# Graph network on Trainium2: picking groups of 13, 12, 12 and 12 nodes, and a third buffer for gathered rows

## The chip, the core and the metric

The kernel runs on one NeuronCore of a Trainium2 chip. The metric is the device time of one execution in microseconds; of several runs the median is taken. The engines are PE (matrix multiplication), DVE (vector), ACT (scalar), POOL (here it issues indirect DMAs, that is gathers and scatters by row) and SP (it issues plain DMAs).

## The reference, cut to what matters

Four graph layers work on 6250 nodes with 32 features and 200000 edges sorted by destination, with a residual and a layer norm after each:

```python
x = layernorm(x + L0(x, edge_attr_32))   # relu(x[src] + e), summed by dst
x = layernorm(x + L1(x))                 # softmax attention by cosine, over edges of a dst
x = layernorm(x + L2(x, edge_attr_2))    # spline convolution, 4 corners an edge
x = layernorm(x + L3(x, edge_attr_16))   # five PNA layers: sum, mean and max by dst
```

For this change only one step of L1 and L3 counts: for each edge, fetch a row of a node table, `table[src[e]]`. In L3 one layer of five is

```python
h   = x[dst] @ P + x[src] @ Q + (edge_attr @ eW + eb) @ C + pb   # 32 values an edge
out = [x, mean_dst(h), sum_dst(h), max_dst(h)] @ poW + pob
x   = relu(out @ lW + lb)
```

so the table is `x @ Q` (TQ), 32 wide, new in every layer. In L1 it is x and one over its norm, 33 wide, fetched once.

## The kernel before, in words

Edges lie as 128 partitions by J = 1568 slots. They are worked in NCH = 28 chunks of C = 56 slots, and one slot is 128 edges. Node n has the high digit n // 49 (0 to 127, its partition in tables held on chip) and the low digit n % 49.

**Two ways to fetch.** Of the 56 slots of a chunk POOL fetches the first 36 in the last layer (20 in L1), each with one indirect DMA of 128 rows from HBM (L1775, L1095). The other KP = 20 (KP1 = 36 in L1) are "picked" by PE and DVE from a table on chip:

- The table is split into three bf16 parts that add up to the f32 value (QS, L2003 to L2013; QS1, L1385 to L1394), and its 49 low digits into PG = 4 groups of PH = 13; 4 x 13 = 52, and the three digits too many are zeros. A part of a group is 32 features by 13 digits, 416 columns (33 by 13, 429, in L1).
- DVE makes one-hots (L2023, L1272): for each group a 128x128 matrix for a slot, a one where the edge's key, group x 128 + high digit, is the row's. Keys come by DMA from a table KG, broadcast to all partitions.
- PE multiplies the one-hot of each group with the three parts of the group, 12 matmuls into one PSUM bank (L1862, L1173). An edge has a one in one group only, so the bank then holds, for each edge, 32 features by 13 low digits of its group.
- DVE multiplies by a mask of the low digit within the group (`by_h`, L2032, L1285; the mask is made by `which`, L2076, from hpb) and reduces over the 13 (`together`, L2037, L1291) into the same buffer where the gathered rows land (G3, G1).

Three PSUM banks turn: pick k starts once the reduction of pick k - 3 is done (of pick k - 2 for the first two picks of a chunk).

**Order on each engine in the last layer.** All of it is written out by hand. PE: 20 picks, after picks 13, 15, 17 and 19 two matmuls each for the edge attributes (`mix`, L1872). DVE: for each pick k by_h(k), together(k-1), one-hots for the next ten picks at k = 0, 2, 4, 6 of ten; between them the work on the chunk before: two adds of gathered and picked rows onto the edge sums in PSUM (`add`, L2046) after picks 2 and 4, four half scans for sum and maximum (L2068) after picks 6, 8, 10 and 12, the next mask after pick 16. ACT copies scans out and lays the edge terms. POOL: the gathers of a chunk, before them a wait until the adds of two chunks before are done, since G3 has two buffers. At the end of each of the five layers the rows are stored, gathered by node, and go through small matmuls to the next table; then DVE's `parts` splits it and PE waits for that.

**L1** is the same with 36 picks; DVE puts the steps of `chunk` between picks 1 and 20, `fill` (a 3.96 us scan, L1307) after pick 23 and cell numbers (`cells_v`) after 26 to 33. POOL also scatters 39 rows of another table in each chunk (L1077).

**Keys.** `pick_keys_v` (L1549) runs once, at the end of L0: q_g is the group number of each edge, q_kf = 128 q_g + high digit goes through PE transposes (L509) to KG, hpb = low digit - 13 q_g is the digit within the group.

Of the kernel before, what the change touches and what calls it, by code (L numbers as in the profile page):

```python
# [19 lines left out]
C = 56  # L20
# [5 lines left out]
PG = 4  # L26
PH = 13
KP = 20
# [47 lines left out]
def program(nc, x, src, dst, ea16, ea2, ea32, eps, beta, w2, root2, bias2,  # L76
            eW, eb, pW, pb, poW, pob, lW, lb, out):
    ctx = ExitStack()
    with ctx:
# [172 lines left out]
        with ExitStack() as ph:  # L252
            NB = sb(ph, "l1n", [128, PG * PH, 34])
# [10 lines left out]
            QS1 = sb(ph, "qs1", [128, PG, 3, 33, PH], BF16)  # L264
            QR1 = [O1[i][:, :, :].rearrange("p a b -> p (a b)")[:, 0:PG * PH * 33].rearrange("p (a b) -> p a b", b=33)
# [53 lines left out]
        with ExitStack() as ph:  # L319
            XC = sb(ph, "xc", [128, NC, 32])  # L320
            PN = RX
            G3 = [sb(ph, f"l3g{i}", [128, C, 32]) for i in range(2)]
# [6 lines left out]
                "p (a b) -> p a b", b=128) for i in range(2)] for t_ in G3)  # L329
            XT = [OF[0][0:32, :, :].rearrange("p a b -> p (a b)")[:, 896 * i:896 * i + 896].rearrange(  # L330
                "p (a b) -> p a b", b=128) for i in range(2)]
            QN = OF[1][:, :, :].rearrange("p a b -> p (a b)")[:, 0:PG * PH * 32].rearrange("p (a b) -> p a b", b=32)
            QR = [O3[1][:, 0:52, :].rearrange("p a b -> p (a b)")[:, 1664 * i:1664 * i + 1664].rearrange(
                "p (a b) -> p a b", b=32) for i in range(2)]
            QS = sb(ph, "qs", [128, PG, 3, 32, PH], BF16)
# [16 lines left out]
        def ranked(r):  # L352
# [27 lines left out]
                   + z1.over(root=2, tab=3, hat=1, tabd=16, hatd=16, sl=16 * NCH, lays=NCH, fm=NCH, filled=NCH,  # L380
                             score=2 * NCH, ev=NCH, em=NCH, av=NCH, spread=NCH, prod=NCH, scan=2 * NCH, lay=3 * NCH,
                             o0=16 * 14, o1=16 * 14, cells=NCH, celld=32 * NCH, lastT=2, fa=1, fea=1, fb=1, feb=1,
                             carry=2, carryT=2, oh=NB1 * NCH, pk=KP1 * NCH, pev=KP1 * NCH, red=RED0 + KP1 * NCH, m5=NCH))

# [689 lines left out]

        def send(e, a, b):
# [39 lines left out]
        def layer1_sp(e):  # L1115
# [24 lines left out]
            e.wait_ge(z1["tab"], 3)  # L1140
# [23 lines left out]
        def layer1_t(e):  # L1164
            e.wait_ge(z1["parts"], 1)
            with nc.Fori(0, 2 * NCH, engines=[e.engine], hint_back_edge=True, head_slot={e.engine: 0}) as i:
                for k in range(KH1):
# [3 lines left out]
                    for g in range(PG):  # L1171
                        for p in range(3):
                            x_ = e.matmul(ps[k % 3][:, 0:33 * PH],  # L1173
                                          OH1[k // SB1][:, g, 128 * (k % SB1):128 * (k % SB1) + 128],
                                          QS1[:, g, p, :, :].rearrange("p f h -> p (f h)"),
# [84 lines left out]
        def layer1_v(e, vc):  # L1260
# [107 lines left out]
            e.memset(NB[:, NC:PG * PH, :], 0.0).then_inc(z1["tab"], 1)  # L1368
# [11 lines left out]
            def by_group(t_):  # L1380
                return t_.rearrange("p (g h) f -> p g f h", g=PG)

            NBt = NB[:, :, 0:33]
            e.wait_ge(z1["tab"], 3)
            a = vc.up(e.tensor_copy(QS1[:, :, 0, :, :], by_group(NBt)).then_inc(vec, 1))  # L1385
            e.wait_ge(vec, a)
            a = vc.up(e.tensor_tensor(by_group(QR1[0]), by_group(NBt), QS1[:, :, 0, :, :], ALU.subtract).then_inc(vec, 1))
# [928 lines left out]
```

## Time and profile before

| what | value |
|---|---|
| median of 3 runs | 15540.85 us (15536.74 to 15546.09) |
| the profiled execution: its time, its span | 15539.17 us, 15537.4 us |
| PE matmul busy | 10581.2 us, 68% |
| DVE busy | 10047.1 us, 65% |
| POOL busy | 10665.1 us, 69% |
| ACT busy | 2687.8 us, 17% |
| mean granted TensorE clock | 0.875 of full |

How to read it: the kernel goes through stages with different limits. L1's picking loop is at 2630 to 5068 us of the span, L2 without picks at 5220 to 8100, and the five last layers from 8116 to 15415. Busy shares of the whole span mix them. A busy PE is modelled: each matmul's duration holds its latency, so the step from one start to the next tells the rate.

### The profile page before, as it was taken

Reading aid. Unit: us, or ns where it says so; the run is one execution under the profiler, and the core shown is the slowest. Engines: PE = TensorE matmul, PEld = TensorE weight load, DVE = VectorE, ACT = ScalarE, POOL = GpSimd, SP = SyncE. Lnnn points to the kernel's source line nnn. Section 1 sums busy time; section 2 is a strip of 40 time slices with the busy share of each in tenths; the row PEclk is TensorE's granted clock in tenths of the full one; section 3 lists DMA queues with packets and bytes.
Section 4 is the critical chain, followed back from the end, with each engine's and each line's share of the span. In section 5 each row is a group of like instructions: output and inputs, shape, how many; then the busy total and the mean of one; then the engine's idle time right before and its main releaser. Section 6 shows DMA issues by size and latency. Waiting matters only on the chain. (4 is left out here: it accounts for less than half of the span.)

```text
span 15537.4 us, 159495 instructions
## 1 busy us (share of the span) xinstructions
PE 10581.2 (68%) x59370; PEld 6309.5 (41%) x59370; DVE 10047.1 (65%) x16354; ACT 2687.8 (17%) x3352; POOL 10665.1 (69%) x10775
## 2 busy tenths in 40 slices
PE   0166562999999540000029997999799979988997
PEld 0155551444444220000015554555455545545554
DVE  2799993777777213333337775777577757776776
ACT  0122221010101100000002221222222212221222
POOL 3777666666666777777767775777577667766775
PEclk9999999999999555555559998999899989998998
DMA  5122222111111222222212221222122212221221
GB/s 195 43 63 63 67 60 48 40 44 40 44 40 40 72 82 69 72 73 71 71 46 74 74 75 52 74 74 74 52 74 73 76 54 74 75 68 57 74 74 60
DMA packets 677474, 1029.59 MB, mean 66 GB/s; under 512 B 252382, under 2 KB 526347, under 8 KB 652027
## 3 DMA queue, kind: packets, MB, share of 16 engines
q1 hardware_dynamic: 311483, 763.42, 13.9%
q0 software_dynamic: 344384, 236.12, 7.5%
q10 hardware_dynamic: 21216, 25.94, 0.5%
q14 instruction: 281, 2.30, 0.0%
q8 instruction: 110, 1.80, 0.0%
HBM read 587.57 MB, written 479.53 MB: 69 GB/s over the span
## 5 line engine op out<-in xcount | busy, mean ns | idle before, releaser
L1862 PE MATMUL ps<-qs,oh 128*128 128x416 bf16 x33600 | 6083.2, 340 | 342.0 <-DVE l3g L2037 269.0
L1775 POOL DMA_INDIRECT l3g<-TQ,srcs x5040 | 4835.2, 959 | 1984.4 <-issue 1510.0
L1862 PEld LDWEIGHTS ps<-qs,oh 128*128 128x128 bf16 x33600 | 3242.8, 98 | 3105.9 <-DVE l3g L2037 518.2
L2032 DVE TENSOR_TENSOR pt<-ps,l3m 128x416 f32<-128x416 f32 x2800 | 1635.3, 584 | 1668.4 <-PE ps L1862 1663.6
L1173 PE MATMUL ps<-qs,l1oh 128*128 128x429 bf16 x12096 | 2282.0, 350 | 261.7 <-DVE l1g L1291 156.5
L967 POOL DMA_INDIRECT l0g<-T,srcs x1568 | 1640.5, 1046 | 847.8 <-issue 487.5
L1077 POOL DMA_INDIRECT T<-p,poss x1568 | 1529.6, 976 | 807.8 <-issue 478.7
L1685 POOL DMA_INDIRECT l2g<-Y,t x1568 | 1680.5, 1072 | 489.6 <-issue 489.6
L1173 PEld LDWEIGHTS ps<-qs,l1oh 128*128 128x128 bf16 x12096 | 1183.8, 99 | 1359.6 <-DVE l1g L1291 211.1
L2037 DVE TENSOR_REDUCE l3g<-pt 128x32 f32<-128x416 f32 x2800 | 1598.2, 575 | 0.0
L1938 ACT COPY l3o<-l3of 128x1792 f32<-128x1792 f32 x280 | 966.3, 3451 | 3189.5 <-DVE l3of L2068 3189.5
L1583 PE MATMUL ps<-ident,qe 128*128 128x128 f32 x196 | 49.1, 429 | 1970.2 <-DMA qe<-U_a 1970.0
L2068 DVE TENSOR_TENSOR_SCAN l3of<-l3mr,psv 128x912 f32<-128x912 bf16 x560 | 1146.3, 2048 | 10.0 <-DVE psv L2053 0.3
L1729 DVE TENSOR_TENSOR l2p<-l2g,l2w 128x3584 f32<-128x3584 f32 x56 | 219.4, 3918 | 1400.5 <-DMA l2g<-Y,t 1400.5
L1285 DVE TENSOR_TENSOR nd<-ps,l1m 128x429 f32<-128x429 f32 x1008 | 606.4, 602 | 542.1 <-PE ps L1173 536.3
L1583 PEld LDWEIGHTS ps<-ident,qe 128*128 128x128 f32 x196 | 38.0, 223 | 1981.3 <-DMA qe<-U_a 1980.4
L1095 POOL DMA_INDIRECT l1g<-T,srcs x560 | 536.2, 958 | 170.6 <-issue 170.6
L1957 ACT COPY psv<-ps 128x512 f32<-128x512 f32 (+1 forms) x560 | 289.4, 517 | 1990.7 <-PE ps L1872 1361.5
L2023 DVE TENSOR_SCALAR oh<-kb,ramp 128x1280 bf16<-128x1280 f16 x1120 | 620.6, 554 | 2.0 <-DMA kb<-KG 2.0
L1291 DVE TENSOR_REDUCE l1g<-nd 128x33 f32<-128x429 f32 x1008 | 592.4, 590 | 0.0
L622 PE MATMUL psv<-bCs,bAT 128*128 128x49 f32 x1568 | 444.9, 423 | 108.0 <-DVE bAT L585 108.0
L638 ACT COPY bCs<-ps 128x49 f32<-128x49 f32 x1568 | 316.3, 202 | 1164.9 <-PE ps L616 1164.3
(396 smaller groups left out, 11083.1 us busy)
## 6 DMA issues: line engine op xcount, KB each, us to landing
W<-l3o SPq DMA_DIRECT2D x140, 1792.0 KB, 5.8
kb<-KG SPq DMA_DIRECT2D x280, 320.0 KB, 3.3
l3g<-TQ,srcs POOLq DMA_INDIRECT x5040
l3t<-AT SPq DMA_DIRECT2D x140, 448.0 KB
bLB<-KT SPq DMA_DIRECT2D x112, 448.0 KB
Y<-yb SPq DMA_DIRECT2D x49, 1024.0 KB, 3.9
l1kb<-KG SPq DMA_DIRECT2D x112, 288.0 KB, 3.4
W<-l1o SPq DMA_DIRECT2D x28, 952.0 KB, 3.7
```

What stands on the lines that cost most here:

```text
L967: e.indirect_dma_start(G0[s][:, j, :], None, T0, bass.IndirectOffsetOnAxis(ap=srcs[:, c * C + j:c * C + j + 1], axis=0)).then_inc(z0[f"g{s ...
L1077: e.indirect_dma_start(T4, bass.IndirectOffsetOnAxis(ap=poss[:, j:j + 1], axis=0), p4[:, j, :], None).then_inc(z1[f"sent{j // 784}"], 16)
L1173: x_ = e.matmul(ps[k % 3][:, 0:33 * PH], OH1[k // SB1][:, g, 128 * (k % SB1):128 * (k % SB1) + 128], QS1[:, g, p, :, :].rearrange("p f h - ...
L1285: e.tensor_tensor(PT1[r % 3], ps[r % 3][:, 0:33 * PH].rearrange("p (f h) -> p f h", h=PH), M51[r // KP1 % 2][:, r % KP1, None, :].to_broad ...
L1685: e.indirect_dma_start(G2[s3][:, j, :, :].rearrange("p a b -> p (a b)"), None, Y, bass.IndirectOffsetOnAxis(ap=t4[:, j0 + j, 1:2], axis=0) ...
L1775: e.indirect_dma_start(G3[s][:, j, :], None, TQ, bass.IndirectOffsetOnAxis(ap=srcs[:, c * C + j:c * C + j + 1], axis=0)).then_inc(z3[f"g{s ...
L1862: x_ = e.matmul(ps[k % 3][:, 0:32 * PH], OH[k // SB][:, g, 128 * (k % SB):128 * (k % SB) + 128], QS[:, g, p, :, :].rearrange("p f h -> p ( ...
L1938: e.copy(O3[i % 2][:, :, 32 * step:32 * step + 32], OF[step][:, :, 1:C + 1].rearrange("p f j -> p j f")).then_inc(z3["lay"], 1)
L2023: x_ = e.tensor_scalar(OH[m % 2][:, g, :], KB[m % 2][:, :], ramp[:, g:g + 1], None, ALU.is_equal)
L2032: e.tensor_tensor(PT[r % 3][:, :, :], bank(r), M5[r // KP % 2][:, r % KP, None, :].to_broadcast([128, 32, PH]), ALU.mult).then_inc(z3["ev" ...
L2037: e.tensor_reduce(G3[r // KP % 2][:, C - KP + r % KP, :], PT[r % 3][:, :, :], AXX, ALU.add).then_inc(z3["red"], 1)
L2068: e.tensor_tensor_scan(OF[step][:, :, :].rearrange("p f j -> p (f j)")[:, x0:x1], MR[step][:, :, :].rearrange("p f j -> p (f j)")[:, x0:x1 ...
```

## The change

The 49 low digits are cut into groups of 13, 12, 12 and 12 and nothing is padded. The parts lie group behind group, each as features by digits of its own group, so the three matmuls of the first group stay 416 (429) columns wide and the nine others are 384 (396). PSUM is still read by DVE as 32 by 13: the narrow matmuls write 12 of each 13 words, and the thirteenth keeps what the first group wrote there. DVE's masks, products and reductions keep their shapes. Splitting takes two instructions (first group, three others) in place of one. The keys use the bounds 13, 25, 37, and hpb is the low digit - 12 q_g, less one where the group isn't the first. In the last layer G3 has three buffers, and the gathers of a chunk wait for the adds of three chunks before.

```diff
-PG = 4
 PH = 13
+GROUPS = ((0, 13), (13, 12), (25, 12), (37, 12))
+PG = len(GROUPS)
...
-            G3 = [sb(ph, f"l3g{i}", [128, C, 32]) for i in range(2)]
+            G3 = [sb(ph, f"l3g{i}", [128, C, 32]) for i in range(3)]
...
-            QS = sb(ph, "qs", [128, PG, 3, 32, PH], BF16)
+            QS = sb(ph, "qs", [128, 3, NC * 32], BF16)
...
+        def by_group(rows, f):
+            n = GROUPS[0][1]
+            return (rows[:, 0:n, 0:f].rearrange("p h f -> p f h"),
+                    rows[:, n:NC, 0:f].rearrange("p (g h) f -> p g f h", g=PG - 1))
+        def in_parts(part, f):
+            n = GROUPS[0][1] * f
+            return (part[:, 0:n].rearrange("p (f h) -> p f h", f=f),
+                    part[:, n:NC * f].rearrange("p (g f h) -> p g f h", g=PG - 1, f=f))
...
                 for g in range(PG):
                     for p in range(3):
-                        x_ = e.matmul(ps[k % 3][:, 0:32 * PH], OH[k // SB][:, g, 128 * (k % SB):128 * (k % SB) + 128],
-                                      QS[:, g, p, :, :].rearrange("p f h -> p (f h)"),
+                        n0, n = GROUPS[g]
+                        x_ = e.matmul(ps[k % 3][:, 0:32 * PH].rearrange("p (f h) -> p f h", h=PH)[:, :, 0:n],
+                                      OH[k // SB][:, g, 128 * (k % SB):128 * (k % SB) + 128],
+                                      QS[:, p, 32 * n0:32 * (n0 + n)].rearrange("p (f h) -> p f h", h=n),
                                       start=g == 0 and p == 0, stop=g == PG - 1 and p == 2)
...
         def pick_keys_v(e, vc):
-            a = vc.up(e.tensor_scalar(q_g, hibs[:, :], float(PH), None, ALU.is_ge).then_inc(vec, 1))
-            for k in range(2, PG):
-                e.wait_ge(vec, a)
-                a = vc.up(e.scalar_tensor_tensor(out=q_g, in0=hibs[:, :], scalar=float(PH * k), in1=q_g,
-                                                 op0=ALU.is_ge, op1=ALU.add).then_inc(vec, 1))
+            a = vc.up(e.tensor_scalar(q_kf, hibs[:, :], float(GROUPS[1][0]), None, ALU.is_ge).then_inc(vec, 1))
+            e.wait_ge(vec, a)
+            a = vc.up(e.scalar_tensor_tensor(out=q_g, in0=hibs[:, :], scalar=float(GROUPS[2][0]), in1=q_kf,
+                                             op0=ALU.is_ge, op1=ALU.add).then_inc(vec, 1))
+            e.wait_ge(vec, a)
+            a = vc.up(e.scalar_tensor_tensor(out=q_g, in0=hibs[:, :], scalar=float(GROUPS[3][0]), in1=q_g,
+                                             op0=ALU.is_ge, op1=ALU.add).then_inc(vec, 1))
+            e.wait_ge(vec, a)
+            a = vc.up(e.scalar_tensor_tensor(out=hpb[:, :], in0=q_g, scalar=-12.0, in1=hibs[:, :],
+                                             op0=ALU.mult, op1=ALU.add).then_inc(vec, 1))
+            e.wait_ge(vec, a)
+            a = vc.up(e.tensor_tensor(hpb[:, :], hpb[:, :], q_kf, ALU.subtract).then_inc(vec, 1))
             e.wait_ge(vec, a)
             e.scalar_tensor_tensor(out=q_kf, in0=q_g, scalar=128.0, in1=lobs[:, :],
                                    op0=ALU.mult, op1=ALU.add).then_inc(kg["split"], 1)
-            vc.up(e.scalar_tensor_tensor(out=hpb[:, :], in0=q_g, scalar=-float(PH), in1=hibs[:, :],
-                                         op0=ALU.mult, op1=ALU.add).then_inc(vec, 1))
...
-                    s = i % 2
-                    if i >= 2:
-                        e.wait_ge(*z3.at("add", 2 * (i - 1)))
+                    s = i % 3
+                    if i >= 3:
+                        e.wait_ge(*z3.at("add", 2 * (i - 2)))
```

The matmul of L1 (L1173) changes in the same way with 33 features. The memsets of the padding in NB (L1368) and QN (L1998) go. Both splits (L1385, L2003) become a loop over the three parts with a cast for each of the two pieces and, for the first two parts, a subtraction for each piece. The buffer that `together` and `add` use is `i % 3`, and the semaphore of the third buffer is one that L1's scatters used.

## Rows read from the trace of the kernel before

**Rows 1.** The page, busy time of the engines: us, share, instructions.
```profile
PE 10581.2 (68%) x59370; PEld 6309.5 (41%) x59370; DVE 10047.1 (65%) x16354; ACT 2687.8 (17%) x3352; POOL 10665.1 (69%) x10775
```

**Rows 2.** Windows: length, busy PE, PEld, DVE, ACT, POOL (instructions), clock, DMA, GB/s.
```profile
2600.00:5080.00 2480.00, 2281.98 (x12096) 1183.77 (x12096) 1863.31 (x3544) 258.16 (x223) 1627.36 (x1675) 0.97 0.17 41
9602.00:10930.00 1328.00, 1270.02 (x7014) 710.74 (x7014) 999.44 (x1569) 323.70 (x214) 959.87 (x1006) 1.00 0.23 71
```

**Rows 3.** The page, groups by line: busy us, mean ns, idle before and its releasers.
```profile
L1862 PE MATMUL ps<-qs,oh 128*128 128x416 bf16 x33600 | 6083.2, 340 | 342.0 <-DVE l3g L2037 269.0
L1173 PE MATMUL ps<-qs,l1oh 128*128 128x429 bf16 x12096 | 2282.0, 350 | 261.7 <-DVE l1g L1291 156.5
```

**Rows 4.** Timeline of PE, a last-layer chunk: start, us, instructions [idle before, releaser].
```profile
10325.55 19.40 PE L1862 MATMUL ps<-qs,oh 128*128 128x416 bf16 x108 [0.75 <-DVE l3g L2037]
10345.56 8.61 PE L1862 MATMUL ps<-qs,oh 128*128 128x416 bf16 x48 [0.61 <-DVE l3g L2037]
10354.78 2.28 PE L1862 MATMUL ps<-qs,oh 128*128 128x416 bf16 x12 [0.61 <-DVE l3g L2037]
...
10373.50 2.81 PE L1862 MATMUL ps<-qs,oh 128*128 128x416 bf16 x15 [0.75 <-DVE l3g L2037]
```

**Rows 5.** Timeline of DVE in the same chunk.
```profile
10333.61 1.69 DVE L2046 TENSOR_TENSOR psv<-psv,l3g 128x896 f32<-128x896 f32 x1
...
10349.99 0.59 DVE L2032 TENSOR_TENSOR pt<-ps,l3m 128x416 f32<-128x416 f32 x1 [0.56 <-PE ps L1862]
10350.50 0.57 DVE L2037 TENSOR_REDUCE l3g<-pt 128x32 f32<-128x416 f32 x1
10351.00 0.54 DVE L2023 TENSOR_SCALAR oh<-kb,ramp 128x1280 bf16<-128x1280 f16 x1
...
10351.70 2.05 DVE L2068 TENSOR_TENSOR_SCAN l3of<-l3mr,psv 128x912 f32<-128x912 bf16 x1
...
10354.15 0.57 DVE L2037 TENSOR_REDUCE l3g<-pt 128x32 f32<-128x416 f32 x1
```

**Rows 6.** Timeline of PE, a chunk of L1.
```profile
3885.78 15.66 PE L1173 MATMUL ps<-qs,l1oh 128*128 128x429 bf16 x84 [1.02 <-DVE l1g L1291]
3901.70 31.07 PE L1173 MATMUL ps<-qs,l1oh 128*128 128x429 bf16 x168 [0.26 <-DVE l1g L1291]
3935.53 24.64 PE L1173 MATMUL ps<-qs,l1oh 128*128 128x429 bf16 x126 [2.76 <-DVE l1g L1291]
```

**Rows 7.** Timeline of DVE, the fill of two chunks of L1 that follow each other.
```profile
3844.54 3.96 DVE L1307 TENSOR_TENSOR_SCAN psv<-nd,psv 128x1824 f32<-128x1824 bf16 x1
...
3929.89 3.96 DVE L1307 TENSOR_TENSOR_SCAN psv<-nd,psv 128x1824 f32<-128x1824 bf16 x1
```

**Rows 8.** Window around PE's stop in L1, columns as in Rows 2.
```profile
3930.00:3945.00 15.00, 12.24 (x61) 6.04 (x59) 11.48 (x21) 0.00 (x0) 11.48 (x12) 0.89 0.17 33
```

**Rows 9.** Timeline of POOL, last layer, two waits a chunk apart.
```profile
10335.67 0.94 POOL L1775 DMA_INDIRECT l3g<-TQ,srcs  x1 [0.30 <-issue]
10339.75 0.94 POOL L1775 DMA_INDIRECT l3g<-TQ,srcs  x1 [3.13 <-DVE psv L2046]
...
10383.60 0.94 POOL L1775 DMA_INDIRECT l3g<-TQ,srcs  x1 [0.30 <-issue]
10387.68 0.94 POOL L1775 DMA_INDIRECT l3g<-TQ,srcs  x1 [3.13 <-DVE psv L2046]
```

**Rows 10.** Waits of POOL: us in total, times, longest us.
```profile
POOL l3g L1775 <- DVE psv L2046: 240.4, 79, 3.1
```

**Rows 11.** Timeline at the end of L0: the key pass and PE's first transpose.
```profile
2510.91 1.79 DVE L1556 SCALAR_TENSOR_TENSOR p<-p,lobs 128x1568 f32<-128x1568 f32 x1
...
2512.84 1.49 PE L509 MATMUL ps<-ident,p 128*128 128x128 f32 x4 [116.38 <-DVE p L1556]
```

**Rows 12.** Timeline of DVE before the first last-layer loop: one cast of a part.
```profile
8103.32 1.75 DVE L2003 CAST qs<-l3of 128x1664 bf16<-128x1664 f32 x1
```

More of the change, by code:

```diff
@@ L1378, in layer1_v @@
                             ALU.mult).then_inc(z1["hat"], 1)
[L1380 to L1385, printed above, removed]
-            e.wait_ge(vec, a)
-            a = vc.up(e.tensor_tensor(by_group(QR1[0]), by_group(NBt), QS1[:, :, 0, :, :], ALU.subtract).then_inc(vec, 1))
-            e.wait_ge(vec, a)
-            a = vc.up(e.tensor_copy(QS1[:, :, 1, :, :], by_group(QR1[0])).then_inc(vec, 1))
-            e.wait_ge(vec, a)
-            a = vc.up(e.tensor_tensor(by_group(QR1[1]), by_group(QR1[0]), QS1[:, :, 1, :, :],
-                                      ALU.subtract).then_inc(vec, 1))
-            e.wait_ge(vec, a)
-            a = vc.up(e.tensor_copy(QS1[:, :, 2, :, :], by_group(QR1[1])).then_inc(vec, 1))
-            e.wait_ge(vec, a)
+            e.wait_ge(z1["tab"], 2)
+            for p in range(3):
+                rows = NB if p == 0 else QR1[p - 1]
+                for to, of in zip(in_parts(QS1[:, p, :], 33), by_group(rows, 33)):
+                    a = vc.up(e.tensor_copy(to, of).then_inc(vec, 1))
+                e.wait_ge(vec, a)
+                if p < 2:
+                    for to, of, less in zip(by_group(QR1[p], 33), by_group(rows, 33), in_parts(QS1[:, p, :], 33)):
+                        a = vc.up(e.tensor_tensor(to, of, less, ALU.subtract).then_inc(vec, 1))
+                    e.wait_ge(vec, a)
             e.sem_inc(z1["parts"], 1)
@@ L2002, in parts @@
                     e.wait_ge(*z3.at("pk", KP * l * NCH))
-                a = vc.up(e.tensor_copy(QS[:, :, 0, :, :], by_group(QN)).then_inc(vec, 1))
-                e.wait_ge(vec, a)
-                a = vc.up(e.tensor_tensor(by_group(QR[0]), by_group(QN), QS[:, :, 0, :, :],
-                                          ALU.subtract).then_inc(vec, 1))
-                e.wait_ge(vec, a)
-                a = vc.up(e.tensor_copy(QS[:, :, 1, :, :], by_group(QR[0])).then_inc(vec, 1))
-                e.wait_ge(vec, a)
-                a = vc.up(e.tensor_tensor(by_group(QR[1]), by_group(QR[0]), QS[:, :, 1, :, :],
-                                          ALU.subtract).then_inc(vec, 1))
-                e.wait_ge(vec, a)
-                e.tensor_copy(QS[:, :, 2, :, :], by_group(QR[1])).then_inc(z3["parts"], 1)
+                for p in range(3):
+                    rows = QN if p == 0 else QR[p - 1]
+                    for to, of in zip(in_parts(QS[:, p, :], 32), by_group(rows, 32)):
+                        i_ = e.tensor_copy(to, of)
+                        if p < 2:
+                            vc.up(i_.then_inc(vec, 1))
+                    if p < 2:
+                        e.wait_ge(vec, vc.n)
+                        for to, of, less in zip(by_group(QR[p], 32), by_group(rows, 32), in_parts(QS[:, p, :], 32)):
+                            a = vc.up(e.tensor_tensor(to, of, less, ALU.subtract).then_inc(vec, 1))
+                        e.wait_ge(vec, a)
+                i_.then_inc(z3["parts"], 1)
             def one_hots(m, groups):
```

36 lines of the change are left out of this document (17 added, 19 removed).

## The prediction

> **What bounds the kernel now.** I read the page's busy shares first. PE is busy 68% of the span and POOL 69% [rows 1], so no engine's total names the bound; the stages have to be taken apart. Two of them run the code that the change touches: the picking loop of the second layer (L1173, microseconds 2630 to 5068) and the five picking loops of the last layer (L1862, 8116 to 15415). In a last-layer loop PE is busy 1270 of 1328 us, DVE 999 and POOL 960; in the second layer's it is PE 2282, DVE 1863, POOL 1627 of 2480 [rows 2]. PE ends last in both, but not by much: the groups by line show that what PE waits for in the last layer is DVE's reduction L2037 [rows 3]. So the question is how much of a shorter matmul reaches the end, and the timeline of one chunk answers it.
>
> Last layer, one chunk (20 picks of 12 matmuls). PE's timeline [rows 4]: a run of 48 matmuls takes 8.61 us. The first ends 0.34 after its start (mean 340 ns, [rows 3]), so start to start is (8.61-0.34)/47 = 0.176 us, and a pick P = 12 x 0.176 = 2.11. PE stands still before pick 9 (10345.56), before pick 13 (10354.78) and before the next chunk (10373.50), and a little within the run of 108 (9 x 2.11 + 0.16 = 19.2 of 19.40, so 0.2: pick 5). Each stop ends with a reduction: pick k needs the reduction of pick k-3. From pick 9 to 13 the path is two picks (4.22), then DVE: it starts on pick 10 at 10349.99, does two one-hot/reduce pairs' worth of work and a 2.05 us scan, and ends the reduction at 10354.15 + 0.57, PE resumes at 10354.78 [rows 4, 5]. That is 2P + 5.00 = 9.22. From 5 to 9 it is the same form (L2068 again), so pick 5 starts at 10336.34, and from 0 to 5 it is 10.79 = 3P + 4.45 (L2046's 1.69 us add at pick 2, [rows 5]). From 13 to the next chunk: 18.72 = 7P + 3.94 (mixing matmuls, and the loop top, which waits for DVE's reduction of the pick before last). Sum: **14P + 18.4** = 47.95 us, which is 10373.50 - 10325.55. Six of twenty picks lie beside DVE.
>
> Second layer, one chunk (36 picks). Start to start is (15.66-0.35-0.03)/83 = 0.184 (0.03 is my estimate of a stop within that run), P1 = 2.21 [rows 6]. From pick 5 to 12: 15.92 = 5P1 + 4.87; from 12 to 26: 33.83 = 12P1 + 7.31, the 7.31 being mostly the 3.96 us scan L1307 [rows 7]. A chunk is 3929.89 - 3844.54 = 85.35 [rows 7], so the rest is 35.6 = 12P1 + 9.1. In that rest PE goes slow for a moment after its 2.76 us stop: 126 matmuls take 24.64, i.e. 0.194 each instead of 0.184, 1.3 us more [rows 6], with a granted clock of 0.89 over those 15 us [rows 8]. Sum: **29P1 + 21.3**.
>
> **The change part by part.**
> Narrow matmuls. What a 384-column matmul costs no row shows. 416 columns at 2.4 GHz are 173.3 ns and measured 176.0, so 2.7 over; 429 are 178.8 and measured 184.1, 5.3 over [rows 4, 6]. I take the same extras: 384 columns 160 + 2.7 = 162.7; 396 columns 165 + 5.3 = 170.3. Then P = 3 x 0.176 + 9 x 0.1627 = 1.99 and P1 = 3 x 0.184 + 9 x 0.1703 = 2.085, 0.120 and 0.124 less. Bounds: below, no extra (P 1.97, P1 2.04); above, nothing saved, or more than that, because these matmuls write PSUM in 32 (33) runs of 12 words with one left out, and every matmul of the kernel so far writes one unbroken run. Nearest to the rows is the value above.
> Last layer: 14 x 0.120 = 1.68 us a chunk, 135 chunks (the first of each layer has no adds and scans: 20 x 0.120 = 2.4, five of them): 227 + 12 = **-239 us**. The six picks beside DVE bring nothing: DVE's chain of adds and scans is late next.
> Second layer: 29 x 0.124 = 3.6 a chunk. Further DVE steps of 2 us stand among its first twelve picks and leave PE a margin of about nothing there (the 0.03 above); with picks 0.12 shorter I let them take 0.3 back. 3.3 x 28 = **-92 us**. The slow moment after the long stop stays, since the stop gets longer; it could cost 1 us a chunk more or go away (bounds +28 and -36).
> POOL, in the last layer: a gather starts every 1.25 us; 36 with two slower ones need 45.1 us a chunk, and POOL waits 2.8 us for L2046 in each [rows 9] (240 us in all, [rows 10]). The wait goes with three buffers. With a chunk of 14 x 1.99 + 18.4 = 46.3 us POOL still has 1.2 to spare, and gathers are used more than half a chunk after they are issued. So the third buffer is worth **0**: it lets POOL run ahead. Without it the result would be the same; if chunks fell under 45.1, POOL would be late next.
> DVE's keys (L1550 on): one more tensor_tensor over 1568 elements, and two passes rather than none now stand ahead of the one that releases PE. PE was waiting there (116 us, L509 on L1556), each pass costs 1.8 [rows 11]. PE's transposes, the store of the keys and, behind them in PE's queue, layer 0's last transpose start later: **+3.6 us** (bounds 0 and +4).
> Splitting into parts: each cast of 1664 elements (1.75 us, [rows 12]) becomes two over 1568. Elements saved 0.1, a second instruction added, about 0.1; five instructions a layer, PE waits for all of them. Take 0 (bounds -0.6 and +1 a layer, 6 layers). The memsets that go are 0.1 us each.
> Semaphores for the third buffer are reused from finished ones, and no queue gets a new instruction ahead of its old ones.
>
> The profiled execution took 15539.17, the median is 15540.85. 15539.2 - 239 - 92 + 3.6 = 15211.8; against the median, **15213**. Measured differences under about 0.2% (31 us) can't be told from none.
>
> **A rule that speaks against it.** The rows show only unbroken outputs, so they can't test this. The Trainium skill (PSUM, Specifications) gives PSUM 8-byte lines and says that any non-contiguous pattern slows matmuls significantly; its Advanced Engine Details and Errata (PSUM Cachelines) says that every two consecutive elements should be contiguous. By the second sentence read word for word the runs of 12 are fine and the sum is mine; by the first it is one of the two rivals that follow.
>
> **The rivals.**
> 1. Broken runs cost what they save. A run starts at word 13f. If outputs go out two words at a time at even places, a run with odd f touches 7 places, not 6: 16 x 6 + 16 x 7 = 208 pairs = 416 columns. The matmul stays at 176 ns, and the time is 15539.2 + 3.6, **15544** against the median. For it: the saving is just one word a run, so a cost of one column a run eats it all. Against: nothing in the rows.
> 2. Slower. Same place, higher price. From 176 ns on for a narrow matmul (one column a run) it is slower than before. At two columns a run it is 162.7 + 27 = 189 ns (198 in the second layer): P = 2.23, P1 = 2.33; +1.68 x 140 and +3.65 x 28 + 4 give **15882**. If every pair of an odd run were split in two, it is 16 x 6 + 16 x 12 = 288 pairs = 576 columns, 243 ns (250): P = 2.71, PE never waits inside the chunk, 20P + 3.9 = 58.1, +10.15 x 140 = 1421; second layer 36 x 2.80 + 2 = 103, +17.5 x 28 = 490: **17460**.
> 3. DVE or POOL holds the pace everywhere. If PE's stops grew by all that is saved, the gain would be the matmuls outside adds and scans alone, 7P and 10P1: 0.84 x 140 + 1.2 x 28 = 152 less 4: **15393**. Against it: DVE itself waits 0.56 us for pick 10 between two scans [rows 5], so it does not run free there.
>
> **How the numbers follow.** Forecast 0.50 (its own range 15135 to 15300: no extras at all give 14 x 0.024 x 140 + 29 x 0.048 x 28 = 86 more; the clock and the parts some 40 either way); rival 3 0.05; rival 1 0.17; rival 2 0.28, about 0.10 of it up to two columns a run. Faster 0.55, same 0.16, slower 0.29. The range reaches from 15140 to the two-column case, 15900, and leaves out the split pairs and a little below.
>
> **What would show it.** In the changed profile: the L1862 row for 128x384 at some 163 ns start to start and chunks of 46.3 us (right); 176 ns (rival 1); 189 or more and PE's waits for L2037 gone (rival 2). PE's stops before picks 5, 9 and 13 should grow by about 0.24 each. Second-layer chunks of 82 us. POOL's waits for L2046 near 0 until late in each layer, with no effect. L509's first start 3.6 us later. I am wrong if a narrow matmul isn't shorter.

## The result, and the profile after

The changed kernel takes **15592.69 us** (median of 6 runs, 15589.39 to 15598.45), the kernel before in the same sitting 15538.22 (6 runs, 15533.62 to 15546.09). The ratio is **1.0035**, 95% interval 1.0022 to 1.0048: slower by 54 us, where the forecast was 15213, faster by 328. The kernels e5 to e13 below were timed where the kernel before itself took 23944 to 24012 us, with PE standing still for some 30 us in the middle of many chunks (why isn't known), so their totals are set beside that figure and never beside 15540.

The changed kernel's busy shares (us, share, instructions) answer to [rows 1]:

```profile
PE 10617.3 (68%) x59370; PEld 6451.4 (41%) x59370; DVE 10063.5 (65%) x16379; ACT 2687.2 (17%) x3352; POOL 10694.5 (69%) x10775
```

Nothing of a pick shorter by 6% is to be seen. If nine of twelve matmuls had become 8% shorter, PE's busy time would have fallen by hundreds of microseconds; it rose by 36. Windows over the two picking loops (length, busy PE, PEld, DVE, ACT, POOL, clock, DMA share, GB/s), the second shifted by 40 us with its loop, against [rows 2]:

```profile
2600.00:5080.00 2480.00, 2300.69 (x11998) 1217.46 (x11999) 1846.02 (x3503) 255.80 (x220) 1620.14 (x1663) 0.98 0.17 41
9642.00:10970.00 1328.00, 1269.87 (x7022) 730.29 (x7023) 999.30 (x1570) 323.77 (x214) 961.48 (x1002) 1.00 0.23 71
```

In the last layer 1328 us hold what they held before (7022 matmuls, 7014 before). In the second layer 98 of the 12096 matmuls are still to come at 5080, where all had run before. Groups by line and form of the changed kernel (busy us, mean ns of one, idle before and its releasers) tell wide from narrow matmuls, against [rows 3]:

```profile
L1875 PE MATMUL ps<-qs,oh 128*128 128x384 bf16 x25200 | 4894.6, 343 | 0.0
L1875 PE MATMUL ps<-qs,oh 128*128 128x416 bf16 x8400 | 1951.7, 341 | 363.3 <-DVE l3g L2047 287.4 <-DVE qs L2015 75.3
L1187 PE MATMUL ps<-qs,l1oh 128*128 128x396 bf16 x9072 | 1910.2, 361 | 0.0
L1187 PE MATMUL ps<-qs,l1oh 128*128 128x429 bf16 x3024 | 731.0, 351 | 249.5 <-DVE l1g L1305 144.6 <-DVE l1oh L1286 104.9
```

This is the view that decides. A matmul of 384 columns takes 343 ns from its start to its modelled end, one of 416 columns 341: the same. In the second layer 396 columns take 361 ns, 10 *more* than 429. PE's timeline of one last-layer chunk (start, us, instructions, idle before), against [rows 4]:

```profile
10363.24 10.72 PE L1875 MATMUL ps<-qs,oh 128*128 128x416 bf16 x60 [0.75 <-DVE l3g L2047]
10374.20 8.61 PE L1875 MATMUL ps<-qs,oh 128*128 128x416 bf16 x48 [0.24 <-DVE l3g L2047]
10383.42 8.61 PE L1875 MATMUL ps<-qs,oh 128*128 128x416 bf16 x48 [0.61 <-DVE l3g L2047]
10392.65 2.28 PE L1875 MATMUL ps<-qs,oh 128*128 128x416 bf16 x12 [0.61 <-DVE l3g L2047]
...
10411.36 8.96 PE L1875 MATMUL ps<-qs,oh 128*128 128x416 bf16 x50 [0.75 <-DVE l3g L2047]
```

(The form named is that of a row's first matmul; wide and narrow alternate within it.) 48 matmuls take 8.61 us, to the hundredth what they took before: start to start 0.176, wide and narrow alike, P = 2.11. The 13th pick waits 0.61 us as before. The stop ahead of pick 5, which in the kernel before lay within the run of 108, stands out now: from the start of the matmul before it to the next start, less the 0.176 of a matmul, it was 0.23 us (median) and is 0.39; the 0.24 of the row counts from the modelled end. A chunk is 10411.36 - 10363.24 = 48.12 us here; over all chunks but the first of each layer the mean is 48.06, and 47.97 in the kernel before. A second-layer stretch of the changed kernel, against [rows 6]:

```profile
3898.98 15.99 PE L1187 MATMUL ps<-qs,l1oh 128*128 128x429 bf16 x84 [0.75 <-DVE l1g L1305]
3915.16 31.81 PE L1187 MATMUL ps<-qs,l1oh 128*128 128x429 bf16 x168 [0.19 <-DVE l1g L1305]
```

168 matmuls take 31.81 us instead of 31.07: (31.81 - 0.36)/167 = 0.1883, P1 = 2.26 instead of 2.21; a chunk went from 85.35 to 86.30 in the mean. Taken apart by a matmul's place in the pick (medians of start to start in the trace), the narrow ones with the first part of the table take 195 ns, with the second 182, with the third 194.

That mean hides two kinds of chunk. In the kernel before every chunk of this loop has the slow moment behind PE's long stop, a stretch at the lower level of TensorE's clock [rows 8]. In the changed kernel 12 of 26 chunks (the first and the last left out) have none and last 85.48 us, and 14 have it and last 86.8 to 87.3. Two windows of 15 us behind the same stop of 2.66 us, one of each kind (columns as in [rows 2]):

```profile
3088.00:3103.00 15.00, 15.00 (x81) 8.09 (x80) 11.21 (x33) 0.00 (x0) 6.84 (x8) 1.00 0.12 29
3516.00:3531.00 15.00, 15.00 (x73) 7.78 (x72) 9.90 (x29) 0.00 (x0) 6.52 (x7) 0.90 0.13 27
```

The granted clock is 1.00 in the first and 0.90 in the second, and the second holds eight matmuls fewer. So the longer matmuls cost some 1.6 us a chunk, 85.33 to about 87, and in 12 chunks the clock gave back about 1.5. What decides it no run shows.

**Where the +50.2 us of the span lie**, from the starts of the first and last matmul of each loop in both traces:

| stretch | before | after | difference |
|---|---|---|---|
| start of the second layer's loop | 2629.9 | 2634.7 | +4.8 |
| that loop | 2438.2 | 2463.6 | +25.4 |
| from there to the first last-layer loop | 3047.6 | 3050.5 | +2.9 |
| five last-layer loops together | 6710.0 | 6720.8 | +10.8 |
| four stretches between them | 589.4 | 597.0 | +7.6 |
| the end | 122.4 | 121.1 | -1.3 |

Half of the loss is the second layer's loop, where the matmuls got longer; the rest are four small bills.

### The profile page after: what moved, and what is told of

Read it like the earlier page. It is cut to its first block and busy times, and to the rows that moved or that the text cites. A ratio compares the mean times of both kernels' runs of the same rounds, so it can differ in the third digit from the quotient of the medians.

```text
span 15587.6 us, 159519 instructions
## 1 busy us (share of the span) xinstructions
PE 10617.3 (68%) x59370; PEld 6451.4 (41%) x59370; DVE 10063.5 (65%) x16379; ACT 2687.2 (17%) x3352; POOL 10694.5 (69%) x10775
## 5 line engine op out<-in xcount | busy, mean ns | idle before, releaser
L1875 PE MATMUL ps<-qs,oh 128*128 128x384 bf16 (+1 forms) x33600 | 6082.1, 342 | 363.3 <-DVE l3g L2047 287.4
L1875 PEld LDWEIGHTS ps<-qs,oh 128*128 128x128 bf16 x33600 | 3339.2, 101 | 3029.9 <-DVE l3g L2047 519.2
L1187 PE MATMUL ps<-qs,l1oh 128*128 128x396 bf16 (+1 forms) x12096 | 2319.4, 358 | 249.5 <-DVE l1g L1305 144.6
L1187 PEld LDWEIGHTS ps<-qs,l1oh 128*128 128x128 bf16 x12096 | 1227.3, 102 | 1341.3 <-DVE l1g L1305 190.3
```

The source lines that it names most:

```text
L1187: x_ = e.matmul(ps[k % 3][:, 0:33 * PH].rearrange("p (f h) -> p f h", h=PH)[:, :, 0:n], OH1[k // SB1][:, g, 128 * (k % SB1):128 * (k % SB1 ...
L1875: x_ = e.matmul(ps[k % 3][:, 0:32 * PH].rearrange("p (f h) -> p f h", h=PH)[:, :, 0:n], OH[k // SB][:, g, 128 * (k % SB):128 * (k % SB) + ...
```

## The experiments

Two theories for the narrow matmul stood at the start. **Place decides:** an output with gaps is written in pairs of words at even places, and each pair touched costs two columns (rival 1's mechanism). **Breaks cost:** each gap has a price of its own, whatever the place. They give the same 176 ns for the changed kernel, so they need other layouts. The first four kernels shared one sitting, in which the kernel before took 15543.11 (15 runs).

**e1_unbroken.** Narrow outputs as one unbroken run; left out is the placing of their values, which land among other digits.

```diff
...
-  ps[k % 3][:, 0:32 * PH].rearrange("p (f h) -> p f h", h=PH)[:, :, 0:n],
+  ps[k % 3][:, 0:32 * n],
... (the second layer in the same way with 33)
```

> The changed kernel, but each narrow matmul writes its 384 (396) columns as one unbroken run from the start of the bank. It leaves out the right places of the groups 1 to 3 in the bank, so sums mix digits; all instructions and shapes on DVE stay. Theory (the broken output costs what the columns save): narrow matmuls start to start at 160 + 2.7 = 163 ns, a chunk of the last layer 14 x 1.99 + 18.4 = 46.3 us, time about 15592.7 - 48.06 x 140 + 46.3 x 140 = 15346 from the last layer alone and some 80 less by the second layer: 15260. Rival (a matmul with its weight load can't go below 176 ns, whatever its width): 176 ns stay, time 15590.

Measured 15201.32, ratio 0.978 (0.9765 to 0.9795). Groups by form, and one row of PE's timeline in the last layer:

```profile
L1875 PE MATMUL ps<-qs,oh 128*128 128x384 bf16 x25200 | 4560.7, 326 | 0.0
L1187 PE MATMUL ps<-qs,l1oh 128*128 128x396 bf16 x9072 | 1728.9, 336 | 0.0
```
```profile
10127.37 8.13 PE L1875 MATMUL ps<-qs,oh 128*128 128x416 bf16 x48 [0.78 <-DVE l3g L2047]
```

343 became 326 ns and 361 became 336, with the same operands and the same columns. Start to start a narrow matmul takes 163 ns, 167 to 171 in the second layer: what the prediction had assumed. A chunk is 46.22 us (the prediction's 14P + 18.4 gives 46.26 with P = 1.99) and the stop ahead of picks 9 and 13 grew from 0.61 to 0.78 and 0.85. So the form of the output alone stood between the forecast and the result: 391 us. The expectation was 59 us too high: the second layer's loop gave 129.5 us (2463.6 to 2334.1) where it had 80.

**e2_pitch_14.** Words of a feature 14 apart instead of 13, so that every run starts at an even word. There are as many breaks in the narrow outputs, and the wide ones now have breaks too.

```diff
...
-  ps[k % 3][:, 0:32 * PH].rearrange("p (f h) -> p f h", h=PH)[:, :, 0:n],
+  ps[k % 3][:, 0:32 * 14].rearrange("p (f h) -> p f h", h=14)[:, :, 0:n],
... (the second layer in the same way with 33; DVE's product reads 13 of each 14 words)
```

> The changed kernel, but a feature's words stand 14 apart in the bank, not 13: every run starts at an even word. Results are right, DVE's shapes stay. Theory A (words go in aligned pairs; a run from an odd word touches one more): narrow matmuls have 6 pairs a run, 384 columns, 163 ns; those of the first group have 7 pairs a run, 448 columns, 186.7 + 2.7 = 189 ns; P = 3 x 0.189 + 9 x 0.163 = 2.03, chunk 46.9 us, last layer -160 us against the changed kernel. Theory B (every break between runs costs a column, wherever it is): narrow 176 ns, first group 416 + 32 columns = 189 ns, P = 2.15, chunk 48.5, last layer +70 us. Rival (floor of 176 ns): 176 or more for all, time 15590 or up.

Measured 15434.48, ratio 0.9931 (0.9915 to 0.9946). Groups by form:

```profile
L1875 PE MATMUL ps<-qs,oh 128*128 128x384 bf16 x25200 | 4571.1, 327 | 0.0
L1875 PE MATMUL ps<-qs,oh 128*128 128x416 bf16 x8400 | 2063.3, 357 | 422.2 <-DVE l3g L2047 338.3 <-DVE qs L2015 75.4
L1187 PE MATMUL ps<-qs,l1oh 128*128 128x396 bf16 x9072 | 1874.2, 355 | 0.0
```

Last layer: 32 runs of 12 words from even places are six pairs each, 384 columns, and take 163 ns start to start, with all their breaks. The wide ones, which had no breaks and 176 ns, are now 32 runs of 13, seven pairs each, 448 columns: 448/2.4 + 2.7 = 189.4, measured 190. Both as place says; a price for breaks is refuted. The chunk is 46.95. The second layer got no faster (P1 = 2.26 as in the changed kernel, a chunk 86.52): the wide ones rose to 195 to 198 ns, 231 pairs, and the narrow ones still take 195 with the first part of the table, 173 to 175 with the second and 187 to 189 with the third, so something besides the output costs there.

**e3_features_inside.** The other way to avoid gaps: in the table's parts and in the bank the digits lie outside and the features inside, so a group of 12 digits is one unbroken run of 12 x 32 words. DVE reads the bank with a step of 32 words in the product instead.

```diff
...
-  ps[k % 3][:, 0:32 * PH].rearrange("p (f h) -> p f h", h=PH)[:, :, 0:n],
+  ps[k % 3][:, 0:32 * n],
...
-  QS[:, p, 32 * n0:32 * (n0 + n)].rearrange("p (f h) -> p f h", h=n),
+  QS[:, p, 32 * n0:32 * (n0 + n)],
...
-  return ps[r % KP % 3][:, 0:32 * PH].rearrange("p (f h) -> p f h", h=PH)
+  return ps[r % KP % 3][:, 0:32 * PH].rearrange("p (h f) -> p f h", f=32)
...
-  return (rows[:, 0:n, 0:f].rearrange("p h f -> p f h"), ...)
+  return (rows[:, 0:NC, 0:f],)
... (in_parts and the second layer in the same way)
```

> The changed kernel with the digits outside and the 32 (33) features inside, in the parts and in the bank: narrow matmuls then write one unbroken run of 384 (396) words with right results, and a part is split by one instruction. DVE's product reads the bank with a step of 32 (33) words. Theory: narrow 163 ns (about 170 in the second layer), DVE's product still 0.58 us, time 15592.7 - 247 (last layer) - 100 (second layer) - 12 (splits): about 15235, faster than before. Rival: DVE's strided read of PSUM costs more than 0.58 us, and DVE becomes the bound; at 0.9 us a product its work in a chunk grows by 6.4 us and the gain goes.

Measured **15164.97**, ratio 0.9759 (0.9744 to 0.9774): faster than both kernels. Views: PE's timeline of a last-layer chunk; two products of DVE; the split of a table into parts; PE in the second layer:

```profile
10090.48 10.12 PE L1871 MATMUL ps<-qs,oh 128*128 128x416 bf16 x60 [0.75 <-DVE l3g L2043]
10100.87 8.21 PE L1871 MATMUL ps<-qs,oh 128*128 128x416 bf16 x48 [0.26 <-DVE l3g L2043]
10109.85 8.13 PE L1871 MATMUL ps<-qs,oh 128*128 128x416 bf16 x48 [0.77 <-DVE l3g L2043]
10118.83 2.16 PE L1871 MATMUL ps<-qs,oh 128*128 128x416 bf16 x12 [0.85 <-DVE l3g L2043]
...
10136.71 1.51 PE L1871 MATMUL ps<-qs,oh 128*128 128x416 bf16 x8 [0.75 <-DVE l3g L2043]
```
```profile
10094.67 0.59 DVE L2038 TENSOR_TENSOR pt<-ps,l3m 128x416 f32<-128x416 f32 x1 [0.87 <-PE ps L1871]
...
10112.66 0.57 DVE L2038 TENSOR_TENSOR pt<-ps,l3m 128x416 f32<-128x416 f32 x1
```
```profile
8002.66 0.98 DVE L2011 CAST qs<-l3of 128x1568 bf16<-128x1568 f32 x1
8003.67 1.79 DVE L2017 TENSOR_TENSOR l3o<-l3of,qs 128x1568 f32<-128x1568 f32 x1
```
```profile
3936.09 29.34 PE L1183 MATMUL ps<-qs,l1oh 128*128 128x429 bf16 x168 [0.33 <-DVE l1g L1301]
```

The stops are e1's, the chunk 10136.71 - 10090.48 = 46.23, and DVE pays nothing for the step: 0.57 to 0.59 us a product [rows 5]. Against e1 it gains 36 us more, which is mostly the split: three casts and two subtractions, 3 x 0.98 + 2 x 1.79 = 6.5 us where the kernel before has 3 x 1.75 + 2 x 2.96 = 11.2. In e1 they take 13.2 (see the parts below), so 6.7 us a layer in six layers, 40 us, are saved against it. The expectation of 15235 had 12 for the splits, and 100 for the second layer's loop, which gave 131 (2463.6 to 2332.3). A second-layer matmul is (29.34 - 0.34)/167 = 0.174 us on average.

**e4_third_buffer.** The kernel before with the third buffer alone.

```diff
-  G3 = [sb(ph, f"l3g{i}", [128, C, 32]) for i in range(2)]
+  G3 = [sb(ph, f"l3g{i}", [128, C, 32]) for i in range(3)]
...
-  if i >= 2: e.wait_ge(*z3.at("add", 2 * (i - 1)))
+  if i >= 3: e.wait_ge(*z3.at("add", 2 * (i - 2)))
... (and i % 3 for i % 2 where the buffer is filled and used)
```

> The kernel before with only the third buffer for gathered rows. Theory (POOL's wait hides nothing that is late): same time within 5 us, POOL's 240 us of waits for L2046 move behind the loop. Rival (gathers that run ahead take memory or DMA time from PE or DVE): up to 10 us slower.

Measured 15551.24 (11 runs, 15540.85 to 15560.67), ratio 1.0005 (0.9996 to 1.0014): no difference that can be told. PE's timeline of a chunk, and POOL's waits (us in total, times, longest):

```profile
10280.52 10.72 PE L1864 MATMUL ps<-qs,oh 128*128 128x416 bf16 x60 [0.75 <-DVE l3g L2039]
10291.48 8.61 PE L1864 MATMUL ps<-qs,oh 128*128 128x416 bf16 x48 [0.24 <-DVE l3g L2039]
```
```profile
POOL l3of L888 <- DMA W<-l3o: 487.9, 5, 98.8
```

POOL's 240 us of waiting for the adds [rows 10] are gone, and come back as a wait at the end of each layer (297.1 in the kernel before, 487.9 here, 512.1 in the changed kernel): POOL arrives earlier and waits for the same store. The chunk, however, has the changed kernel's 0.24 us stop ahead of pick 5 and is 48.08 long instead of 47.97; the five loops together take 6721.5, 11.5 more than in the kernel before. So that stop belongs to the third buffer and not to the matmuls.

**e8_odd_start.** e1 with the last layer's narrow outputs moved by one word, unbroken from an odd place. For this and the kernels that follow it is the length of a matmul, within the long rows of PE's timeline, that can be set beside those above.

```diff
-  ps[k % 3][:, 0:32 * n],
+  ps[k % 3][:, int(g > 0):32 * n + int(g > 0)],
```

> As the unbroken kernel (narrow outputs as one run, digits mixed in the sums), but the narrow outputs of the last layer start at word 1 of the bank, not 0. Theory A (words are merged by their place): 193 pairs, 386 columns, 160.8 + 2.7 = 163.5 ns and 15205 us. Theory B (columns go out in fixed twos, and a two across a pair's border is written twice): 384 pairs, 320 ns and over 18000 us.

```profile
14904.04 8.21 PE L1875 MATMUL ps<-qs,oh 128*128 128x416 bf16 x48 [0.25 <-DVE l3g L2047]
14913.07 6.17 PE L1875 MATMUL ps<-qs,oh 128*128 128x416 bf16 x36 [0.81 <-DVE l3g L2047]
```

48 matmuls take 8.21 us in this row, as in e3's second: 163 ns a narrow one. One unbroken run pays at most one pair for an odd start; the price is one pair a *run*, not one a pair. Measured 23646.14 in total (2 runs), a ratio of 0.9874 (0.9856 to 0.9892) to the kernel before beside it.

**e6_even_parts_l1, e10_even_parts, e12_even_parts.** One kernel, timed three times: the changed kernel with one element of padding ahead of the narrow groups. In the changed kernel a part of the second layer's table is 49 x 33 = 1617 elements, so the narrow groups of the first and third parts start at an odd element (429, 3663) and those of the second at an even one (2046). That is the pattern 195/182/194. Here they all start at even elements.

```diff
-  QS1 = sb(ph, "qs1", [128, 3, NC * 33], BF16)
+  QS1 = sb(ph, "qs1", [128, 3, NC * 33 + 1], BF16)
...
-  QS1[:, p, 33 * n0:33 * (n0 + n)].rearrange("p (f h) -> p f h", h=n),
+  QS1[:, p, 33 * n0 + (g > 0):33 * (n0 + n) + (g > 0)].rearrange("p (f h) -> p f h", h=n),
```

> The changed kernel with one unused element put behind the first group of each part in the second layer, so that every moving operand there starts at an even bf16 element; outputs stay 12 of 13 words. In the changed kernel the narrow matmuls of the second layer take 195, 182 and 194 ns for the parts 1, 2, 3, and the starts of the parts 1 and 3 are odd. Theory (rows of 12 bf16 from an odd element touch 7 two-element words, 33 x 14 = 462 columns, 192.5 + 2.7 = 195; from an even one the broken output rules, 428 columns, 181): all narrow ones at 181 to 182 ns, a pick 2.18 us, chunk 29 x 0.08 = 2.3 us shorter than 86.3, about 15592.7 - 65 = 15528. Rival (the parts' place in SBUF doesn't matter, e.g. the third part is slow for another reason): 188 ns on average, 15592.

> The changed kernel with one element of padding, so that each part of the second layer's gathered rows starts at an even element. Theory 'a bfloat16 row that starts at an odd element touches one two-element word more': the narrow matmuls of the second layer go from 195/182/194 to 181 to 182 ns, a pick from 2.26 to 2.17 us, 29 picks x 28.5 chunks x 0.09 = 74 us less work on TensorE: the time goes from 15593 to about 15520. Theory 'the second layer's rise is the broken output': no change, 15593.

> The changed kernel with the second layer's parts at even elements, once more, on a chip on which the kernel before takes 15.54 ms if there is one. Theory 'a row of the moving operand that starts at an odd element costs one word': TensorE's work of the second layer falls by 29 picks x 28.5 chunks x 0.09 us = 74 us against the changed kernel and by some 33 us against the kernel before (pick 2.17 instead of 2.21): time about 15520. Theory 'chunks of the second layer are paced by something else': 15593.

PE's timeline in the second layer (of e10):

```profile
4082.26 30.60 PE L1188 MATMUL ps<-qs,l1oh 128*128 128x429 bf16 x168 [2.67 <-DVE l1g L1306]
```

168 matmuls take 30.60 instead of 31.81 us: (30.60 - 0.35)/167 = 0.1811, P1 = 2.17. By place in the pick the narrow ones take 181 to 182 ns (177 for the first after the wide ones), where the changed kernel has 195, 182 and 194. So the start of the moving operand costs, and this is shown.

How it costs is worked out, not tested by itself, and the expectation's "rows of 12" put it wrongly. The trace records the moving operand of these matmuls as one unbroken run of 396 elements, also where the kernel's text has rows of 12. And e1, whose moving operands are the same elements at the same odd places, takes 168 ns with the first part where the changed kernel takes 195. An odd start is dear only where the *output* has gaps. A count that fits: each run of the output takes its 12 columns from the moving operand, and from an odd element they lie in seven two-element words, 33 x 7 = 231 words = 462 columns, 192.5 + 2.7 = 195. From an even one six words do, and the output rules with 17 x 6 + 16 x 7 = 214 pairs = 428 columns, 178.3 + 2.7 = 181. In e2 the same count gives 195, 168 and 195 ns for the three parts; measured were 195, 175 and 187, one by one not the same but together 557 for 558.

The kernel's time did not fall: 23949.2, 24016.0 and 24022.93 us, ratios to the kernel before of 1.0004 (0.9995 to 1.0013), 1.0004 (0.9995 to 1.0013) and 1.0007 (0.9998 to 1.0017). What the even starts are worth beside 15540 us wasn't measured.

**e5_two_buffers, e9_two_buffers.** e3 with two buffers for gathered rows, that is e4's edit undone in it.

> The version with the features inside, with the third buffer taken away again (POOL waits for the adds of two chunks before). Theory: its chunk of 46.22 us is still longer than POOL's 45.1, so two buffers do: 15165 within 10 us, chunks of 46.2 us, POOL waits about 1 us a chunk. Rival (POOL's wait plus its gathers exceed the chunk and gathered rows come late): chunks of 47 us or more, 15270.

> The kernel with the features inside (words of a part outside its digits) and two buffers for the last layer's gathered rows, beside the kernel before; its sister with three buffers took 15165. Theory 'the third buffer is worth nothing or costs a little': the release of a buffer then waits for VectorE's product, POOL's wait for it is some 80 us a loop as in the kernel before, and the time is 15155 to 15170. Theory 'the third buffer keeps the shorter chunk (46.2 us) fed': without it the gathers start later and the picks wait, time above 15200 and chunks over 46.5 us. The narrow matmuls keep 163 ns in both.

Measured 23605.62, ratio 0.9856 (0.984 to 0.9871), and 23630.11, ratio 0.9845 (0.9832 to 0.9859). Narrow matmuls take 163 ns in both. No kernel with three buffers that was timed beside them differs from them by the buffer alone. The nearest is e8, timed with e5 and 40.5 us slower: it has e1's layout, which cost 36 us against e3's, one odd word and the third buffer. That leaves some 4 us for the last two, too little to tell from none.

**e7_all_together, e11_all_together, e13_all_together.** e3 with two buffers, even starts in the second layer, and the keys' extra passes behind the release.

```diff
-  a = vc.up(e.scalar_tensor_tensor(out=hpb[:, :], in0=q_g, scalar=-12.0, ...).then_inc(vec, 1))
-  e.wait_ge(vec, a)
-  a = vc.up(e.tensor_tensor(hpb[:, :], hpb[:, :], q_kf, ALU.subtract).then_inc(vec, 1))
-  e.wait_ge(vec, a)
   e.scalar_tensor_tensor(out=q_kf, in0=q_g, scalar=128.0, ...).then_inc(kg["split"], 1)
+  a = vc.up(e.scalar_tensor_tensor(out=hpb[:, :], in0=q_g, scalar=1.0, in1=hibs[:, :], op0=ALU.is_ge, op1=ALU.subtract).then_inc(vec, 1))
+  e.wait_ge(vec, a)
+  a = vc.up(e.scalar_tensor_tensor(out=hpb[:, :], in0=q_g, scalar=-12.0, in1=hpb[:, :], ...).then_inc(vec, 1))
...
-  QS1[:, p, 33 * n0:33 * (n0 + n)],
+  QS1[:, p, 33 * n0 + (g > 0):33 * (n0 + n) + (g > 0)],
```

> Features inside, two buffers, even starts for the second layer's parts, and the two passes for the digit within the group put behind the pass that releases PE. Theory: 15165 less 4 for the keys, and a narrow matmul of the second layer from 169.5 to 168 ns, 9 x 1.5 x 29 x 28 = 11 us less: about 15150, first pick of the second layer 3.6 us earlier than with the features inside alone. Rival (the odd starts cost nothing where the run is unbroken): 15161.

> Features inside, two buffers, the second layer's parts at even elements, and the three extra passes of the key build put behind the release that the first pick of the second layer waits for. Against 15165 for the features inside alone: narrow matmuls of the second layer 168 instead of 168 to 171 ns (some 29 x 28.5 x 0.01 = 8 us), start of the second layer 3.6 us earlier: about 15150. If the parts' start matters nothing once the output is unbroken, 15160.

> Features inside, two buffers, the second layer's parts at even elements and the keys' extra passes behind the release, once more. Against 15165 for the features inside with three buffers: 8 us from the narrow matmuls of the second layer, 3.6 us from the keys, up to 10 us from the two buffers: 15145 to 15155. If the third buffer was worth something with the shorter chunks: 15165 or above.

Measured 23583.48, 23641.31 and 23651.71 us; ratios 0.9848 (0.9834 to 0.9861), 0.9846 (0.9833 to 0.986) and 0.9854 (0.9838 to 0.9871). In the second layer of e11:

```profile
4084.53 31.20 PE L1188 MATMUL ps<-qs,l1oh 128*128 128x429 bf16 x180 [2.90 <-DVE l1g L1306]
```

(31.20 - 0.35)/179 = 0.172 a matmul. A pick takes 2.054 us where e3's takes 2.063, that is 1 ns a narrow matmul, where 1.5 was expected. Why isn't shown: one word for an odd start would give it only in part, and in e3 the second part, which starts even, is with 167 to 171 ns no faster than the odd first part with 168. The keys' edit does what it should: counted from DVE's first instruction of the key block, PE's first transpose starts at 6.6 us in all three, as in the kernel before, where the changed kernel has 10.25. In total e7 is 22 us faster than e5, and e11 11 us slower than e9; so no gain over e3 is shown, and **e3 is the best version measured**.

## Why the prediction was wrong

**The step that failed** is the first: "I take the same extras: 384 columns 160 + 2.7 = 162.7; 396 columns 165 + 5.3 = 170.3", with "nearest to the rows is the value above". The terms -239 and -92 hang on it. It measured 176 and 182 to 195. The extras were not the trouble: e1 gives 163 and 167 to 171 once the output is unbroken. The trouble is that time goes by the pairs of words touched, not by the columns: 16 x 6 + 16 x 7 = 208 pairs = 416 columns = 176 ns, for 384. That is rival 1, to the nanosecond in the last layer; e2 and e8 show that it is this mechanism and not some price for breaks that comes out alike. I had given it 0.17 against 0.50. The prediction noted that every row of the trace shows an unbroken output and then took the nearest row all the same; nearness in columns says nothing about a form that no row has, and the word "nearest" hid that. The Trainium skill's sentence that I read in the change's favour (Advanced Engine Details and Errata, PSUM Cachelines: every two consecutive elements should be contiguous) is met by all runs of 12, and yet they take 176 ns for 163. The Trainium skill's page PSUM — Partial Sum Buffer (Specifications: any non-contiguous pattern slows matmuls significantly) pointed the right way for this change and is too broad: e2's 384-column outputs have gaps and run at 163 ns.

**The rest of the sum**, by its steps:

- *The path through a chunk, 14P + 18.4 and 29P1 + 21.3:* right. With P = 1.99, e1's and e3's chunk is 46.22 where it gives 46.26. Second layer: 81.58 in e1 where the forecast had 82; its loop lost 104 us (2438.2 to 2334.1; forecast 92), the five last-layer loops 249 (forecast 239). Had the outputs been unbroken, the prediction would have been 12 us too high (15213; e1: 15201), and that is in part luck: the loops gave 22 us more than forecast, and some 11 of it went ahead of them and between them, where the forecast had +3.6 for the keys and 0 for the splits.
- *Second layer:* neither my sum nor rival 1 had a term for the moving operand. Parts that start at an odd element, beneath an output with gaps, made P1 2.26 instead of 2.21: with the clock's share, +25.4 us, half of the loss. e6 shows it for the matmul's length; how the odd start costs is worked out only.
- *The slow moment, "stays", bounds +28 and -36:* it went away in 12 of 26 chunks, about 1.5 us each. With it in all of them the changed kernel would have been some 18 us slower still (an estimate, 12 x 1.5).
- *Third buffer, 0:* right within what the runs can tell (e4: 1.0005, interval around 1). It costs about 0.1 us a chunk by the longer stop ahead of pick 5, and with it the +10.8 of the five loops (e4, with no other edit: +11.5). DVE's one-hots between those picks (L2023 before) take 554 ns in the mean in the kernel before, 566 in e4 and 565 in the changed kernel, so a slower DVE is the likely link; why POOL's running ahead should make it so wasn't tried.
- *POOL's wait for L2046:* gone with no effect, as said; the time reappears at the end of each layer (POOL's waits of the changed kernel):

```profile
POOL l3of L888 <- DMA W<-l3o: 512.1, 5, 102.8
```

- *Keys, +3.6:* right. DVE's timeline, and PE's first transpose after it, against [rows 11]:

```profile
2512.34 1.79 DVE L1565 SCALAR_TENSOR_TENSOR hpb<-p,hibs 128x1568 bf16<-128x1568 f32 x1
2514.16 1.79 DVE L1568 TENSOR_TENSOR hpb<-hpb,p 128x1568 bf16<-128x1568 bf16 x1
2515.99 1.79 DVE L1570 SCALAR_TENSOR_TENSOR p<-p,lobs 128x1568 f32<-128x1568 f32 x1
```
```profile
2517.92 1.49 PE L511 MATMUL ps<-ident,p 128*128 128x128 f32 x4 [120.34 <-DVE p L1570]
```

  Two passes of 1.8 more stand ahead of the release; PE starts 5.1 us later than in [rows 11], 3.6 of them the passes, 1.4 a start of DVE's whole block that was already later.
- *Parts, 0 (bounds -0.6 and +1 a layer):* wrong beyond its bound. DVE before the first last-layer loop, against [rows 12]:

```profile
8134.47 2.52 DVE L2015 CAST qs<-l3of 128x416 bf16<-128x416 f32 x2
8137.02 2.85 DVE L2021 TENSOR_TENSOR l3o<-l3of,qs 128x416 f32<-128x416 f32 x2
```

  The two pieces of a cast take 2.52 us where one took 1.75. 3 x 0.77 - 2 x 0.11 is +2.1 a layer; the table above shows +1.9 for each of four and, with one-time costs, +2.9 ahead of the first. I had reasoned from the count of elements, and these passes go by form: e3's unbroken cast of the same elements takes 0.98.
- *Rival 3* is refuted by e1 and e3: stops grew by 0.17 to 0.24 us where a pick got 0.12 shorter, and the path followed the formula. *Rival 2*, more than one column a run at the output, occurs in neither loop; in the second layer the narrow matmuls with an odd start did come to two columns a run, 195 ns, but by the moving operand: with even starts they are at 181.

What stays open: what even parts, and the third buffer beside chunks of 46 us, are worth in the kernel's time; why an odd start costs as it does; and what brings TensorE's slow moment or leaves it out.

## What to carry to other kernels

Before making an operand smaller by leaving words out of a pattern, ask where each run starts: count the aligned pairs that it touches at the output, and, where the output has gaps, look whether the moving operand starts at an even element. Cutting runs of 13 words to 12 at a step of 13 saved nothing; a step of 14 brought 109 us, and a layout in which the part left out lies at the end and the run is unbroken 378 (DVE took the step for nothing). Where no row of a trace shows a form, measure that form alone before counting on it: the changed kernel beside one with an unbroken output would have shown the 391 us that lie between two cases of the prediction.

## What the runs showed of the hardware

- A matmul's f32 output with gaps goes by aligned pairs of words: 32 runs of 12 at a step of 13 take 176 ns (208 pairs), at a step of 14 from even places 163 (192 pairs), 32 runs of 13 at a step of 14 190 (224 pairs). Unbroken, 384 columns take 163 ns from an even or an odd place.
- Where a start at an odd element of the moving bf16 operand costs, it does so together with gaps in the output: 396 columns written as 33 runs of 12 at a step of 13 take 194 to 195 ns from an odd element and 181 to 182 from an even one (changed kernel, e6, e10, e12); written as one run they take 167 to 171 from either (e1, e3).
- Start to start a matmul of the last layer took two columns for each pair touched at 2.4 GHz, plus 2.5 to 2.7 ns, at a granted clock of 1.00 (163 and 176 ns; 190 where the count gives 189). In the second layer that holds for 181, and for 195 with the worked-out count of 231 words; unbroken ones of 396 columns take 167 to 171 where it gives 168, and the kernel before's 429 columns at 184 are 2.6 above it, which no run explains.
- PE's stop of about 2.7 us in each second-layer chunk was followed by a stretch at TensorE's lower clock in 14 chunks of the changed kernel and by none in 12; with it 15 us have a mean granted clock of 0.90.
- A product of DVE that reads PSUM with a step of 32 words takes as long as one with step 1 (0.57 to 0.59 us for 416 elements). A cast of 1568 elements into bf16 takes 0.98 us when both sides are unbroken; with features and digits swapped between the sides it takes 2.52 in two pieces, and 1.75 for 1664 elements in one.
